# A graph network's fused edge loop: where the addresses of products, gathers and bank copies are worked out, and from how many register loads

## The reference

```python
edge_index = jnp.stack([src, dst])
x = _layernorm(x + _L0_gnn_ref(x, edge_index, edge_attr_40, edge_weight, node_type_119, node_vec, ...), axis=-1)
x = _layernorm(x + _L1_gnn_ref(x, edge_index), axis=-1)                      # 5 steps with degree weights
x = _layernorm(x + _L2_gnn_ref(x, edge_weight, src, dst), axis=-1)           # 10 steps with edge weights
x = _layernorm(x + _L3_gnn_ref(x, edge_weight1, ..., src, dst, edge_type_8), axis=-1)
```

```python
gate = jax.nn.silu(edge_attr @ F1W + F1b) @ F2W + F2b
gate = gate + (emb[atom_z[src]] * (emb[atom_z[dst]] @ adapt)).sum(-1, keepdims=True)
msg = gate * h[dst] * (cw * node_mult[dst])[:, None]
agg = jax.ops.segment_sum(msg, src, num_segments=N)
```

## Time and profile before

| what | value |
|---|---|
| runs | 10169.16, 10167.79 and 10154.54 us |
| median | 10167.79 us |
| the profiled execution | 10149.78 us, of which the span is 10148.0 us |
| PE busy | 7475.8 us (74%), weight loads 5850.9 us (58%) |
| VectorE busy | 5440.0 us (54%) |
| GpSimd busy | 5066.9 us (50%) |
| ScalarE busy | 3421.9 us (34%) |
| granted TensorE clock, mean | 0.83 of full speed |
| DMA | 168 GB/s on average over the span |

### The profile page before, as it was taken

How to read it: one execution, slowest core, us unless ns; L and a number is a source line. 1 busy time by engine, 2 the same in 40 slices (tenths; PEclk the granted TensorE clock), 3 DMA queues, 4 the chain that set the end, 5 groups by cost and what they waited for, 6 DMA issues and landing times. The chain is left out here.

```text
span 10148.0 us, 325152 instructions
## 1 busy us (share of the span) xinstructions
PE 7475.8 (74%) x108355; PEld 5850.9 (58%) x108356; DVE 5440.0 (54%) x18470; ACT 3421.9 (34%) x11841; POOL 5066.9 (50%) x6598
## 2 busy tenths in 40 slices
PE   1888865777777776996799499779958789973333
PEld 1555543555555565996699499669933344443333
DVE  7555555444444445998899799889941100012222
ACT  3222212444444443674477267447710000000000
POOL 0677773333333332553355155335537566747776
PEclk9999998666776777998899699889979999965555
DMA  8222222333333223995699299569948799931112
GB/s 327 56 62 62 62 60 93 129 128 135 134 123 136 97 87 99 258 263 139 191 265 264 68 260 263 140 189 263 264 169 321 303 372 368 356 120 21 21 21 20
DMA packets 1592522, 1702.10 MB, mean 168 GB/s; under 512 B 1260587, under 2 KB 1275323, under 8 KB 1546777
## 3 DMA queue, kind: packets, MB, share of 16 engines
q1 hardware_dynamic: 1234710, 1415.38, 44.1%
q10 hardware_dynamic: 252000, 210.40, 6.2%
q0 software_dynamic: 105248, 68.78, 3.7%
HBM read 1331.34 MB, written 361.02 MB: 167 GB/s over the span
## 5 line engine op out<-in xcount | busy, mean ns | idle before, releaser
L1778 POOL TENSOR_TENSOR m_passing<-m_passing 128x196 f32<-128x196 f32 x1488 | 762.5, 512 | 1825.2 <-ACT m_passing L1760 1747.1
L1204 PE MATMUL s_gotd<-m_table_d,s_hot 128*128 x17856 | 1365.1, 205 | 206.6 <-DMA s_hot<-OHT 195.5
L1760 ACT ACTIVATE m_passing<-s_gotd,s_es 128x49 f32<-128x49 f32 x5952 | 1304.4, 303 | 48.6 <-ACT s_es L1753 0.3
L1204 PE MATMUL s_gotq<-m_table_s,s_hot 128*128 x17856 | 1280.9, 185 | 5.6 <-issue 5.6
L1204 PEld LDWEIGHTS s_gotd<-m_table_d,s_hot 128*128 128x128 bf16 x17856 | 990.1, 96 | 289.3 <-DMA s_hot<-OHT 196.9
L1460 POOL TENSOR_TENSOR b_words<-b_words,b_rec 128x512 f32<-128x512 bf16 x372 | 389.5, 1047 | 1517.7 <-DVE b_words L1503 1517.7
L2045 POOL DMA_INDIRECT REC<-m_sums x800 | 956.7, 1196 | 352.1 <-issue 344.6
L483 POOL DMA_INDIRECT REC<-rec,place x800 | 964.1, 1205 | 260.7 <-issue 236.8
L1811 DVE TENSOR_REDUCE s_tops<-s_mt 128x512 f32 (+1 forms) x1488 | 1013.8, 681 | 3.7 <-PE s_mt L1721 3.6
L2078 PE MATMUL p_acc<-p_row,p_feats 128*64 128x512 f32 (+1 forms) x4032 | 902.2, 573 | 146.2 <-DMA p_row<-ADJ 145.4
L1204 PEld LDWEIGHTS s_gotq<-m_table_s,s_hot 128*128 128x128 bf16 x17856 | 992.9, 97 | 4.7 <-issue 4.7
(11 more groups left out here) (475 smaller groups left out, 17288.5 us busy)
## 6 DMA issues: line engine op xcount, KB each, us to landing
s_hot<-OHT SPq DMA_DIRECT2D x1488, 384.0 KB, 3.9
p_row<-ADJ SPq DMA_DIRECT2D x288, 1600.0 KB
s_rec<-REC SPq DMA_DIRECT2D x1488, 98.0 KB, 3.7
OHT<-b_turned ACTq DMA_DIRECT2D x372, 384.0 KB, 2.4
ADJ<-b_acc SPq DMA_DIRECT2D x25, 3200.0 KB, 11.5
REC<-fill SPq DMA_DIRECT2D x124, 624.0 KB, 8.8
b_rec<-REC ACTq DMA_DIRECT2D x372, 108.0 KB, 2.5
p_held<-ADJ ACTq DMA_DIRECT2D x14, 1600.0 KB, 34.4
```

The source lines that it names most:

```text
L1204: last = nc.tensor.matmul(out, hot, table[k][:, bass.ds(at, w)], start=(k == 0), stop=(k == 2))
L1760: last = nc.scalar.activation(msg[:, b % KEPT, j], gotd[b % KEPT][:, j, SW:2 * SW], ACT.Copy, scale=es[:, b % 2, j:j + 1])
L1778: nc.gpsimd.tensor_tensor(rest[:, b % KEPT].rearrange("p g w -> p (g w)"), msg[:, b % KEPT].rearrange("p g w -> p (g w)"), upper(msg[:, b ...
```

## The change

Seven edits, nearly all in build_pass:

1. **One table, one register load.** `lands` moves behind `where`, so a turn has eight words in a row (WHERE = 2 * G) and PE loads all of them at once; the second load is gone. The words of `lands` are packed by multiplication with FIRST and 2 * P: the column in a bank, the half to clear times FIRST, the sums' flag times 16 * FIRST.
2. **landings**, a new stage of PE, stands behind `turn` and works out from these words every address that the four tiles' products and clears need, and keeps them in registers (`pe.to_reg`). `products` then has no register operation between its matmuls.
3. **addresses** of the gathers moves ahead of `products`.
4. **ScalarE's places.** A turn has LEAVES = 8 words, of which six are read in one load by `ways_out`, which is now a stage of its own right behind `take_turned` and keeps the finished addresses. `keep_sums` has no load of its own; `acc` and the banks are addressed through flat views.
5. **store_turned** stores two turns at once, in every second turn: one transfer of 768 KB in place of two of 384 KB, with half as many semaphores.
6. **sources** is one operation of 128 x 512 in place of four of 128 x 128.
7. **Room.** `s_tops`, `s_key`, `s_prod` of the attention pass and `root` of the propagation lie in `passing`, in place of tiles of their own.

```diff
-WHERE = G
+WHERE = 2 * G
+LEAVES = 8
+PSUM_AT = 1 << 25
...
-                ch.step(v.scalar_tensor_tensor(sblk[:], sblk[:], 8.0, first[0], ALU.mult, ALU.add))
+                ch.step(v.scalar_tensor_tensor(sblk[:], sblk[:], float(FIRST) / (2 * P), first[0], ALU.mult, ALU.add))
+                ch.step(v.tensor_scalar(sblk[:], sblk[:], float(2 * P), None, ALU.mult))
...
                 def ways_out(n, b, lap):

                     _, values = nc.values_load_multi_w_load_instructions(
-                        mem["leaves"][0:1, bass.ds(n * 4, 4)], engines=[act.engine], min_val=0,
...
+                        mem["passing"][0:1, bass.ds(n * LEAVES, LEAVES - 2)], engines=[act.engine], min_val=0,
...
+                    for x in banks:
+                        act.to_reg(x * 4 + bank_at)
+                    for x in units:
+                        act.to_reg(x * 4 + acc_at)
+                    act.to_reg(sums_at * 4 + sums_base)
+                    kept = act.snap(values[5] & 31).with_bounds(min_val=1, max_val=NB)
+                    at[b] = banks, units, sums_at, kept
...
                 def store_turned(n, b, lap):
+                    if b % 2 == 0:
+                        return
...
-                    act.dma_start(mem["OHT"][bass.ds(n, 1)].rearrange("g p c -> p (g c)"),
-                                  turned[:, b % TURNED].rearrange("p g k c -> p (g k c)")
-                                  ).then_inc(s_oht[b % TURNED], 16)
+                    first = (b - 1) % TURNED
+                    act.dma_start(mem["OHT"][bass.ds(n - 1, 2)].rearrange("g p c -> p g c"),
+                                  turned[:, first:first + 2].rearrange("p n g k c -> p n (g k c)")
+                                  ).then_inc(s_oht[first // 2], 16)

                 def keep_sums(n, b, lap):
-                    sums_place(n, b, lap)
+                    sums_at = (NB - 1) * SW if isinstance(n, int) and n + 3 >= NG else at[(b + 3) % SLOTS][2]
                     act.wait_ge(s_agg, n + 1)
-                    nc.scalar.copy(sums_flat[:, bass.ds(at["sums", b], SW)], agg).then_inc(s_part, 1)
+                    act.sem_inc(s_load, 1)
+                    nc.scalar.copy(sums_flat[:, bass.ds(sums_at, SW)], agg).then_inc(s_part, 1)
...
-                laps(act, [(load, 0), (take_turned, LEAD), (store_turned, LEAD), (keep_sums, LEAD + 4),
-                           (move_out, LEAD + 1), (embeddings, LEAD + 1)], SLOTS)
+                laps(act, [(load, 0), (take_turned, LEAD), (ways_out, LEAD + 1), (store_turned, LEAD),
+                           (keep_sums, LEAD + 4), (move_out, LEAD + 1), (embeddings, LEAD + 1)], SLOTS)
...
-                        at[b], lands[b] = load_places(nc, mem, n), load_lands(n)
+                        at[b] = load_places(nc, mem, n, 2 * G)

+                def landings(n, b, lap):
+
+                    slots, opens = [], []
+                    for j, x in enumerate(at[b][G:]):
+                        parts = x // FIRST
+                        slots.append(pe.snap(x - parts * FIRST).with_bounds(min_val=0, max_val=FIRST - 2 * P))
+                        if j == 0:
+                            fresh = pe.snap(parts // 16)
+                            parts = parts - fresh * 16
+                            opens.append(fresh.with_bounds(min_val=0, max_val=2 * AGG))
+                        opens.append(pe.snap(parts).with_bounds(min_val=0, max_val=2 * RING + 2))
+                        pe.to_reg(slots[j] * 4 + bank_at)
+                        pe.to_reg((slots[j] + P) * 4 + bank_at)
+                    for x in opens[0 if past(n, 3) else 1:]:
+                        pe.to_reg((x * (2 * P)) * 4 + bank_at)
+                    lands[b] = slots, opens
...
                 def products(n, b, lap):
                     pe.wait_ge(s_high, n + 1)
+                    slots, opens = lands[b]
                     for j in range(G):
-                        slot = pe.snap(lands[b][j] & 7).with_bounds(min_val=0, max_val=7)
-                        clear(pe.snap((lands[b][j] >> 3) & 15).with_bounds(min_val=0, max_val=2 * RING + 2))
+                        slot = slots[j]
+                        clear(opens[j - G])
...
-                laps(pe, [(own_offsets, 1), (turn, 0), (owned, 1), (add, 4), (products, 1), (addresses, 1),
+                laps(pe, [(own_offsets, 1), (turn, 0), (landings, 1), (owned, 1), (add, 4), (addresses, 1), (products, 1),
                           (gathers, 1), (offsets, 0)], SLOTS)
...
-                    for j in range(G):
-                        v.tensor_scalar(turned[:, b % TURNED, j, 2], mem["iota_bf"][:],
-                                        rec[:, b, j, SL - CW:SL - CW + 1], None, ALU.is_equal)
+                    v.tensor_tensor(turned[:, b % TURNED, :, 2], mem["iota"][:].unsqueeze(1).to_broadcast([P, G, P]),
+                                    rec[:, b, :, SL - CW:SL - CW + 1].to_broadcast([P, G, P]), ALU.is_equal)
...
-        tops_at = -(-nc.sbuf_base // 32) * 32
-        tops = room.sb("tops", [P, NG], BF16)
+        used = 2 * ring + ring // 2
+        key, prod = (shared[:, used + k * G * SW:used + (k + 1) * G * SW].rearrange("p (g w) -> p g w", g=G)
+                     for k in range(2))
+        used += 2 * G * SW
+        tops_at = mem["passing_at"] + 4 * used
+        tops = shared[:, used:used + NG // 2].bitcast(BF16)
```

85 lines of the change are left out of this document (40 added, 45 removed).

## The result

The changed kernel is slower: 10,254.92 us (median of four runs, 10,245.74 to 10,259.95) against 10,165.14 us (median of four, 10,154.54 to 10,169.16), a ratio of 1.0092 with a 95% interval of 1.0079 to 1.0104: 0.9% slower, a small difference but clear of the noise. I had forecast 9,545 us.

A forecast was written before the change was run, and what follows sets the result against it. PE's queue, not its array, was taken to set the build turn. Build laps saved 627 us, turns outside the loop 36, attention cost 40: 623 us off 10149.8, plus 18 for the median, gave 9,545 us; range 9,420 to 9,820.

The forecast's parts named there:

- the term for PE's queue in the build turn: Build loop, PE's queue: 5.5 - 2.3 - 0.49 - 0.15 + 1.35 = 3.9 us a turn, with 2.3 for the products.
- a ring of 4.6 us: Build loop: PE's own array work a turn at clock 0.69, the upper bound of a PE-bound turn.
- the queue's 3.9: Build loop: time of PE's instruction queue a turn after the change, 3.9 us, holding at the full clock.
- the kin's price: Build loop, landings: nine operations at the gather addresses' 0.15 us each, 1.35 us; bounds 1.0 and 2.7.
- When the holes close, the granted clock should not fall.: Build loop, PE: clock stays at least 0.69, so 4.6 us of PE work bounds a PE-bound turn from above.
- two of the signs: Build stretch, signs of being right: product loads under 0.45 us apart, 4.3 us turns, 0.2 us PE branch, clock above 0.69.
- rival A: Build loop: branches stay long at 1,708 and 233 instructions, 165 us back, 9,710 us; chance 0.27.
- rival B: Build loop: ScalarE's register load waits for the long copy, a turn needs 5.0 us, 255 us more, 9,800 us; chance 0.15.
- the four rings: Build loop: PE's array 4.6, PE's queue 3.9, ScalarE 3.7 and VectorE's ring 3.5 us a turn.
- the 4.3 of the forecast: Build loop: forecast turn of 4.3 us, above the longest queue because the rings are close.
- top, not the queue, is last: Attention loop: one more operation ahead of gather_tops mostly hides behind top, so 40 us between ends 0 and 179.
- rival C: Whole kernel slower: attention's 179 us paid in full, build turn stays at 5.67 us, about 10,310 us; chance 0.03.

The follow-up runs named there:

- s_tops: a_tops with each later tile's landing ahead of its own products and the gathers' addresses behind the products: 9,683.75 us, ratio 0.9525 to the kernel before.
- h_tops: a_tops with next turn's landings and register load between products and gathers, gathers' addresses behind the transposes: 9,727.17 us, ratio 0.9571 to the kernel before.
- a_addr: Changed kernel with the gathers' addresses back behind the products: 10,170.23 us, ratio 1.0011 to the kernel before.
- c1: a_tops with first landing and load between products and gathers, other landings ahead of their products, gathers' addresses behind transposes: 9,614.86 us, ratio 0.9457.
- a_1611: Changed kernel without the second of each tile's two 128-column products (output not the reference's): 10,192.2 us in one run.
- a_half: Changed kernel without both 128-column products of each tile (output not the reference's): 9,905.03 us, ratio 0.9748 to the kernel before.
- a_act: a_single with ScalarE's register loads where they were, one word and six words in place of one load: 10,186.33 us.
- a_single: Changed kernel with one 384 KB store each turn in place of 768 KB every second turn: 10,185.77 us, ratio 1.0023 to the kernel before.
- a_tops: Changed kernel with the attention tops' address prepared in the form the product uses, saving one operation: 10,114.05 us, ratio 0.9953 to the kernel before.
- h_tops_single: h_tops with one 384 KB store each turn in place of 768 KB every second turn: 9,735.87 us, ratio 0.9578 to the kernel before.

## Why the prediction was wrong

The direction and the size were wrong. The step that failed is the term for PE's queue in the build turn: 2.3 us taken off for the products, where 0.95 came off, and landings that were to run beside the transposes, where they lengthened the turn by 1.1 us. Then the attention rounds cost 123 us where the sum had 40. Point by point, by its own steps:

**"Removed: 2.5 us between the products, of which 0.2 stays for handing over."** This is the step that failed most. The holes between the products closed, but the products take 1.30 us on average and not 0.2: the array needs 0.92 us for them at the full clock and 1.59 at the half one. The term of 2.3 us measured 0.95. The holes between weight loads, on which the prediction rested, are not all idle time of the array. I had counted the array's work elsewhere, as a ring of 4.6 us to be compared with the queue's 3.9, and taken the larger of the two. But queue and array work side by side only while the array has something in hand. In PE's own part the turn is the array's time plus all register time that meets an empty array, and the landings meet one.

**"Landings 1.35 us, and run while the transposes do."** The nine operations took 1.67 us, above the kin's price and within the bounds (1.0 to 2.7). The transposes cover 0.4 us of it, and the segment grew by 1.1 us. Where they stand decides, as s_tops and h_tops show: the same number of operations elsewhere makes the turn outside the branch 0.9 and 1.4 us shorter. Of this some 0.2 to 0.3 us belongs to the gathers' addresses, which moved too (a_addr), and h_tops moved the register load as well.

**"The addresses moved ahead, without the 0.60 us hole."** The hole behind the products went (0.66 to 0.09 us) and one of 0.3 us came ahead of them. a_addr shows that this part of the change is a loss of 0.22 us a turn once the products are bound by the array.

**"One register load with its ALU step, 0.49 us."** Eight words in one load take 593 ns, two loads of four 2 x 330. The load's time goes by the words, not by the loads: 0.07 us, and not 0.33.

**"When the holes close, the granted clock should not fall."** Its mean rose, to 0.74, which hides what counts: it is full in the hole and half in the work behind it. In s_tops and c1, whose holes are spread out, it is 0.85 and 0.88 with more matmuls done. So two of the signs that I had named for being right, no hole between the products' weight loads and a clock above 0.69, came true in a kernel that is slower: neither looks at where the time goes next.

**The branches.** The forecast had them gone. ScalarE's went. PE's did not, with 1,708 records in a lap, and got longer. This was rival A, which I gave 0.27. (ScalarE's loops have 346 and 251 records in the traces, where the prediction counted 322 and 233.)

The Trainium skill, page "Runtime: NRT & Kernel Launch", section "Instruction fetch mechanics", gives PE 2,048 instructions on chip in blocks of 256, and a stall where the target of a branch is not in the current window of two pages. My reading, that a PE loop keeps its target if it is under the 2,048 by one block, does not hold here: 1,612 records (a_1611) stalled in each lap. A window of two such blocks does not fit either, since the 1,492 records of a_half never stalled.

**ScalarE and VectorE as what is late next.** ScalarE: rival B is refuted for this kernel. The load behind the copy takes 0.75 us at the median and ends before the copy does in 87% of the turns (a few loads take up to 3 us), and a_act shows over 1 us more of its queue for nothing. Whether the four rings lie between 3.5 and 4.6 us no run measured one by one. c1, with the operations placed otherwise, has turns of 4.2 us, so none of them is longer than that there; that this is close to the 4.3 of the forecast is no merit of the sum, whose terms were wrong. In s_tops VectorE's words end the idle time ahead of the transposes in 74 of 339 turns, but c1 has the same work on VectorE and shorter turns, so VectorE's work alone does not bound s_tops.

**The attention loop.** That one more operation stands in the chain was forecast, its size was wrong: 40 us forecast, 128 worked out from the trace and 123 measured. The argument "PE's load starts 0.05 us behind top's end and so top, not the queue, is last" holds for an operation that stands ahead of the wait. The new one carries the wait itself, so its time comes behind top in 96% of the turns.

The outcome is the neighbour of rival C, with its two parts: most of the attention's full price (123 of 179 us), and a build turn that hardly moves, far below the 0.48 us from which the change would have paid. It moved by 0.12. I gave it 0.03. Its price was also added up wrongly: 179 us less the 40 of the forecast went onto the time of today, which has no such 40 in it; with the branches as they are it would be 10,168 + 179 = 10,347 us. The cause that I named for the second part, the array at the half clock, is one of three: the uncovered landings and the branch are the others. What a_single gained beyond the branch stays open.

## What to carry to other kernels

A register operation in an engine's queue costs little or nothing where the engine still has work in hand, so addresses that are worked out ahead belong behind the issue of long work, or are best spread between it. Gathered in one block behind short work they cost most of their time, here 1.1 us a turn of the 1.5 that the closed holes had saved; the addresses ahead of the products and longer gathers took the rest. When holes between matmuls are removed, add what the array itself needs for them, at both levels of the clock, before booking the hole as a gain. To see whether queue or array sets the pace, compare the same stretch in turns at the full and at the half clock. And when a tile moves into another one, look whether addresses prepared by hand still have the form in which they are used, and on which instruction the wait stands: one operation behind a wait cost 123 us.

## What the runs showed of the hardware

The time of a register load on PE goes with its words: 330 ns for four and 593 for eight at the median (before and after), about 0.07 us each.

PE's branch to the head of the build loop takes either 0.2 us or 3.4 us and more, and nothing between. In the trace of the transfers a lap with a long branch has eight to ten fetches of 16 KB for PE's queue, and one with a short branch has none. Size alone does not tell which: 1,492 records in a lap gave only short branches (a_half), 1,612 only long ones (a_1611), and at 1,707 or 1,708 seven kernels had only long ones (after, a_tops, a_addr, a_single, a_act, h_tops, h_tops_single), s_tops 8 of 28 and c1 20 of 28. The page's line on the queues of instructions shows the sum, before, a_half and s_tops:

```profile
q8 instruction: 355, 5.82, 0.2%
```

```profile
q8 instruction: 98, 1.61, 0.1%
```

```profile
q8 instruction: 172, 2.82, 0.1%
```

At some 5 us a lap that is up to 140 us of this kernel. What decides it at 1,708, and where between 1,492 and 1,612 the long branches begin, no run here settles.
